# Loading the keys of a batch key head by key head in the second attention of a two-layer transformer

## What is computed

```
draft = einsum('bhqd,bhkd->bhqk', qr, kr) + causal
_, idx = top_k(draft, 128)
mask = full(neg); mask[idx] = 0; mask = where(future, neg, mask)
attn = softmax(draft / sqrt(16) + mask)
out = (attn @ v) @ Wo.T
```

## Time and profile before

| | |
|---|---|
| median of three runs | 2333.65 us |
| profiled execution | 2337.67 us |
| its span | 2335.8 us |
| TensorE busy | 1884.8 us, 81% |
| VectorE busy | 1568.4 us, 67% |
| ScalarE busy | 1180.0 us, 51% |
| GpSimd busy | 791.7 us, 34% |
| second attention with items 0 to 15 | about 1137 to 2109 us of the span |

### The profile page before, as it was taken

The page is one execution under the profiler, slowest core; times in us unless marked ns, Lnnn a source line. Parts: engine busy times, 40 slices in busy tenths (PEclk is TensorE's granted clock), DMA queues, the critical chain, the costliest instruction groups (busy, mean ns, idle before and its releaser), DMA issues. The chain is left out here.

```text
span 2335.8 us, 27456 instructions
## 1 busy us (share of the span) xinstructions
PE 1884.8 (81%) x8426; PEld 1377.3 (59%) x8426; DVE 1568.4 (67%) x3640; ACT 1180.0 (51%) x2963; POOL 791.7 (34%) x511
## 2 busy tenths in 40 slices
PE   5899999899998689997557776855877777677997
PEld 4777777777777568886534443432544434345885
DVE  3677777777777645556337888967888987822335
ACT  3556556556565332323355667645666676152221
POOL 3445545445454246553310111130211111132442
PEclk9999999999999889998756689977878887887998
DMA  4112111121110122221710000023000000001111
GB/s 154 32 44 69 66 51 54 52 79 49 43 65 24 62 81 88 101 81 58 134 29 14 15 14 1 1 28 41 5 16 9 14 15 14 1 1 46 55 41 50
DMA packets 48261, 104.71 MB, mean 45 GB/s; under 512 B 6032, under 2 KB 30992, under 8 KB 43664
## 3 DMA queue, kind: packets, MB, share of 16 engines
q1 hardware_dynamic: 48144, 103.40, 14.9%
HBM read 96.04 MB, written 7.34 MB: 44 GB/s over the span
## 5 line engine op out<-in xcount | busy, mean ns | idle before, releaser
L206 PE MATMUL PS<-XT,AR 128*128 128x512 f32 x2472 | 619.3, 405 | 25.7 <-POOL AR L813 12.3
L206 PE MATMUL PS<-AR 128*128 128x512 f32 (+2 forms) x2568 | 544.0, 366 | 24.8 <-POOL AR L323 13.1
L206 PEld LDWEIGHTS PS<-XT,AR 128*128 128x128 f32 x2472 | 470.6, 193 | 138.6 <-issue 16.5
L206 PEld LDWEIGHTS PS<-AR 128*128 128x128 f32 x2568 | 443.9, 193 | 119.5 <-issue 16.8
L1274 POOL TENSOR_TENSOR AF<-AF 128x512 f32<-128x512 f32 (+3 forms) x64 | 148.4, 2319 | 773.8 <-DVE AF L1474 773.8
L1229 ACT ACTIVATE AF<-PS 128x512 f32<-128x512 f32 x160 | 91.8, 596 | 329.7 <-PE PS L1113 190.0
L1416 DVE MAX8 BF<-PS 128x8 f32<-128x256 f32 (+2 forms) x384 | 195.8, 552 | 33.5 <-PE PS L1103 22.1
L1082 PE MATMUL PS<-AR,XT 48*128 48x128 f32 (+3 forms) x256 | 95.1, 458 | 146.1 <-DVE BF L1340 53.4
L1128 PE MATMUL PS<-AF,BF 128*128 128x512 f32 x320 | 190.9, 707 | 24.3 <-ACT AF L1229 24.3
L567 POOL TENSOR_TENSOR AF<-AF 128x512 f32<-128x512 f32 (+1 forms) x64 | 107.5, 1680 | 168.5 <-DVE AF L698 168.5
L1082 PEld LDWEIGHTS PS<-AR,XT 48*128 48x128 f32 x256 | 52.3, 243 | 185.2 <-issue 76.2
(11 more groups left out here) (173 smaller groups left out, 3516.4 us busy)
## 6 DMA issues: line engine op xcount, KB each, us to landing
AF<-in_mean_w SPq DMA_DIRECT2D x48, 448.0 KB, 3.3
AF<-in_ffn_w SPq DMA_DIRECT2D x14, 1536.0 KB, 6.5
AF<-in_attn_w SPq DMA_DIRECT2D x9, 1536.0 KB, 7.4
XT<-rope_scratch SPq DMA_DIRECT2D x192, 64.0 KB, 2.9
AF<-in_attn_w SPq DMA_DIRECT2D x9, 1024.0 KB, 5.2
AF<-in_ffn_w SPq DMA_DIRECT2D x11, 769.0 KB, 4.2
rope_scratch<-BF SPq DMA_DIRECT2D x20, 256.0 KB, 2.3
AR<-rope_scratch SPq DMA_DIRECT2D x24, 128.0 KB, 4.9
```

The source lines that it names most:

```text
L206: last = nc.tensor.matmul(dst, lhs(a, c), rhs(m, c), start=(first and k == 0), stop=(k == 3 * n - 1 and not more))
```

## The change

SyncE asks for an item's queries first and then for its keys, where before the keys came first. The keys are loaded key head by key head: for each of the four g, SyncE waits until head 4g+3 of the item two before has read its keys (`keys_read(x - 2, 4g + 3)`), and then issues six transfers of 32 KB. So each of items 0, 1, 8 and 9 has 24 key transfers and not 6. Each key head has a semaphore of its own; TensorE waits for it at each `scores(x, q)`, and GpSimd waits for all four before it negates.

```diff
-        def keys_read(x):
+        def keys_read(x, h=15):
 
-            return (listed(x, 15, 1) if tile_of(x)[1] > 0 else scored(x, 15)) + 1
+            return (listed(x, h, 1) if tile_of(x)[1] > 0 else scored(x, h)) + 1
...
                 if x >= 3:
                     sp.wait_ge(A1["ring_full"], keys_read(x - 3))
-                if n % QT == 0:
-                    if x >= 2:
-                        sp.wait_ge(A1["ring_full"], keys_read(x - 2))
-                    for low in (0, 64):
-                        for a, s in enumerate((0, 1, 0)):
-                            src = scr[b, 4, s].rearrange("(c h) t -> c h t", c=HD1)
-                            sp.dma_start(f32(kst[low + a * HD1:low + (a + 1) * HD1, 4 * hf:4 * hf + 4]),
-                                         src[:, 4 * hf:4 * hf + 4]).then_inc(A1[f"kst{hf}"], 16)
                 for low in (0, 64):
                     for j in range(2):
                         for a, s in enumerate((0, 0, 1)):
                             src = scr[b, 2 * hf + j, s].rearrange("(c h) t -> c h t", c=HD1)
                             sp.dma_start(f32(qst[x % 3][low + a * HD1:low + (a + 1) * HD1, 8 * j:8 * j + 8]),
                                          src[:, :, i * P:(i + 1) * P]).then_inc(A1[f"qst{x % 3}"], 16)
+                if n % QT == 0:
+                    for g in range(4):
+                        if x >= 2:
+                            sp.wait_ge(A1["ring_full"], keys_read(x - 2, G1 * g + G1 - 1))
+                        for low in (0, 64):
+                            for a, s in enumerate((0, 1, 0)):
+                                src = scr[b, 4, s].rearrange("(c h) t -> c h t", c=HD1)
+                                sp.dma_start(f32(kst[low + a * HD1:low + (a + 1) * HD1, 4 * hf + g]),
+                                             src[:, 4 * hf + g]).then_inc(A1[f"kst{hf}{g}"], 16)
...
+                pe.wait_ge(A1[f"kst{hf}{q}"], 96 * (n // QT + 1))
                 if q == 0:
-                    pe.wait_ge(A1[f"kst{hf}"], 96 * (n // QT + 1))
                     pe.wait_ge(A1[f"qst{x % 3}"], 16 * 12 * (x // 3 + 1))
...
-                pool.wait_ge(A1[f"kst{hf}"], 96 * (b + 1))
+                for g in range(4):
+                    pool.wait_ge(A1[f"kst{hf}{g}"], 96 * (b + 1))
```

More of the change, by code:

```diff
@@ L965, in build_kernel @@
         A1 = names("a1", "raw_qkv", "raw_wo", "wq_hi", "wq_lo", "wk_hi", "wk_lo", "wv_hi", "wv_lo", "wo_hi", "wo_lo",
-                   "tables", "vproj", "v", "vz", "stored0", "stored1", "kst0", "kst1", "qst0", "qst1", "qst2", "mask", "mask_r",
+                   "tables", "vproj", "v", "vz", "stored0", "stored1", "kst00", "kst01", "kst02", "kst03",
+                   "kst10", "kst11", "kst12", "kst13", "qst0", "qst1", "qst2", "mask", "mask_r",
                    "ring_full", "ring_free", "kneg", "above", "tiny", "stat", "nmax", "thr", "acc", "cut", "tau",
```

## The result

The kernel after takes 2328.20 us, the median of 12 runs (2323.24 to 2332.74), beside 2337.33 us for twelve runs of the kernel before (2333.04 to 2345.21): a ratio of 0.9958 [0.9944, 0.9971], or 9.8 us less [6.8, 13.1]. Run again in the study (`a1_after_again`) it gave 0.9952 [0.9931, 0.9974]. The profiled execution took 2323.24 us with a span of 2321.4, so 14.4 us less in both than the profiled one of before.

What follows compares the result with a forecast made beforehand. Second attention was taken as bound by TensorE's two in-order stalls on loads at the change of batch. -22.8 + 10.1 = -12.7 us from 2337.67 gives 2325.0; lowered by 4.0 for the runs' median, 2321 us, range 2313.5 to 2329.5.

Steps and rivals of the forecast that it cites:

- The stalls: Items 8 and 9, change of batch: TensorE's two waits for loads go, 10.25 and 12.58 us, together -22.8 us.
- Rival (d): Change of batch: a transfer or the score-bank ring still holds `scores(8, 0)`, one stall stays; 2331 to 2334 us; chance 0.05.
- The start: Batch 0: 72 transfers instead of 36 on SyncE's queue move `scores(2, 0)` from 1174.09 to 1184.2, +10.1 us.
- the spacing: SyncE's queue at the start: small key transfers issue 0.442 us apart, as the old ones; bounds 0.35 and 0.643.
- The reading that carried the sign: Start of the stage: transfer engines' time goes with the bytes, about 0.25 us for 32 KB against 0.98 for 128 KB.
- rival (b): Start: a small key transfer holds the engines as long as a large one; +9.6 us, 2343 us; chance 0.05.
- the backlog that was to disappear: Key transfers at the start: landings, up to 5.8 us behind issue before, come 2.8 us after issue.
- (a): Start: small transfers issue 0.35 us apart, so it costs only 5.7 us; -17.1 us, 2316.5 us; chance 0.13.
- (c): Start: small transfers issue 0.643 us apart like the query's, costing 19.8 us; -3.0 us, 2330.6 us; chance 0.07.
- Passed on in full: From `scores(2, 0)` to item 2's search: TensorE's order leaves no idle time, so all +10.1 us arrives.
- The small edits: More waits on TensorE, GpSimd and SyncE, 36 more issues under lists at the batch change: 0, at worst 1 us.
- 3 us of clock: TensorE's granted clock behind the removed stalls: counted 0, with 3 us kept for the range's fast end.

Runs made afterwards that it cites:

- e7: Changed kernel with batch 0's key transfers halved again, 48 of 16 KB per item: 1.0056 of the kernel before.
- e3: Changed kernel with two key heads per transfer at batch 0, 12 of 64 KB per item: 0.9902 of the kernel before, 0.9898 when run again.
- e1: Changed kernel with batch 0 loaded as before the change, batch 1 as after it: 0.9906 of the kernel before, 22.0 us less.
- e2: Changed kernel with batch 1 loaded as before the change, batch 0 as after it: 1.0057 of the kernel before, 13.3 us more.
- b1: Changed kernel whose start leaves out unread query rows and loads upper key rows later: 0.9884 of the kernel before, 0.9897 when run again.
- b2: The lean-start kernel (unread query rows left out, upper key rows later) with GpSimd's negation cut into one per key head: 0.9896 of the kernel before.
- e4: Kernel before with only the order changed at batch 1, queries ahead of whole keys: 0.9934 of the kernel before, 15.4 us less.
- e5: Kernel before with only the split at batch 1, key head by key head ahead of the queries: 0.9989 of the kernel before, 2.6 us less.
- e6: Changed kernel with batch 0's keys in six 128 KB transfers per item, issued by ScalarE's queue: 0.9938 of the kernel before, 14.5 us less.

## Why the prediction was right

**The stalls.** -22.8 was forecast. The waits of the two casts fell by 22.83 us, and the two intervals by 22.67 (19.6 to 24.0 in the other executions with both parts of the edit). Every step held: the scores behind the last list, cast 1.10 us behind the last instruction of `cut`, `scores(8, 1)` 7.4 us behind the cast (6.8 forecast). ScalarE's count for item 7 ended at 1541.14, 4.2 us behind the cast and ahead of the transposes, so nothing took the stalls' place. Rival (d) fell.

**The start.** +10.1 was forecast, +11.3 measured. The mis-sized term is the spacing: from the first key issue to the next query issue 24 transfers take 1156.36 - 1145.09 = 11.27 us, 0.470 each and not 0.442; 48 x 0.028 = 1.3 us covers the difference. The trace of before had it. I divided the first of its two groups at the start by six and left out the gap behind it; the second group is longer:

```profile
1148.12 2.90 SPq L1039 DMA_DIRECT2D AR<-rope_scratch  x6
1151.06 24.30 SPq L1045 DMA_DIRECT2D XT<-rope_scratch  x38
```

From the start of a key group to the start of what follows, (1140.37 - 1137.68 + 1151.06 - 1148.12) / 12 = 0.469 us.

The reading that carried the sign, that a small transfer doesn't hold the engines as a large one does, was right, and too cautious (1.9 us to land, not 2.8): rival (b), which needed 0.78 us each and landings that climb, fell with the change's own rows (0.47 us apart, 2.6 us at most to land) and again with e7, which halved the transfers without any backlog. That 12 of the 36 more issues were nearly free was inside the forecast, in the backlog that was to disappear; e3 shows it. Neither (a) nor (c) came: the form issues in 0.42 us at the median, as the old one did.

**Passed on in full.** The prediction argued this from TensorE's own order; e1, e2, e3 and e7 show it for a start from +0.3 to +33.8 us, within the 4 to 5 us of their intervals.

**The small edits** at 0: items 2 to 5 pass their casts in 0.86 us less than before, so 48 met waits of TensorE cost nothing that shows. The negation of item 1's keys is done at 1176.82 + 5.36 = 1182.18 (forecast 1182), before item 2's scores. It was hidden, but not without effect, which the prediction didn't see: VectorE's instruction of 16 elements was held for 2.61 us and ended 0.03 us behind it. It cost nothing because TensorE waited for item 2's queries until 1185.03; in b1, with a shorter start, a hold of this kind, 5.30 us long, cost about 3.5 us (32.8 against 29.2 in b2).

**The sum.** -12.7 against a profiled -14.4 and a measured -9.8 [-13.1, -6.8]. With the measured start it is -22.8 + 11.3 = -11.5, inside the intervals of both measurements. Of the profiled -14.4 some 3 us lie in stretches for which the prediction had counted 0 (-0.86 in items 2 to 5, -2.1 behind the change of batch); it had kept 3 us of clock for the range. The absolute time, 2321.0 forecast and 2328.2 measured, is 7.2 off, and half of that is not the change: I moved the sum down by 4.0 us for a median of three runs of before, and the median of twelve is 2337.33, at the profiled execution. The profiled execution of after is the fastest of its twelve, which is why it shows more than the medians do. The measured time lies only 1.3 us inside the upper end of the range (2329.5), an end that was set for rival (c), which didn't come: with a base 3.7 us too low the absolute time came close to falling outside, although the mechanism held. The difference to before is the better test, and there the forecast lies 2.9 us from the measured value, inside its interval.

## What to carry to other kernels

- A wait on one product may be a wait on what is queued ahead of it: read the in-order engine's last instruction before the gap, not the releaser's name, and ask which transfers stand behind the buffer's last reader.
- Splitting a load pays where its issues lie under other work. Where they don't, it is free only until the queue and no longer the transfers is the limit, and costs one issue each from there on. Split for the one place, keep it whole for the other; move first what depends on nobody, as order alone gave 13 of the 23 us, and the split alone 3 to 4.
- A spacing is read over all groups of its kind, from the start of one to the start of what follows: the first group alone was 6% short.

## What the runs showed of the hardware

- A second issuing queue added no bytes: 130 and 115 GB/s with two, 132 with one. Item 0's queries landed up to 14.1 us behind their issue and not 5.8. The same key transfers took 0.61 us each to issue on ScalarE's queue, beside 0.42 on SyncE's.
- The busy share of the transfer engines doesn't go with the bytes: from 1144 to 1154 it was 1.20 at 132 GB/s before, with keys of 128 KB, and 0.48 at 125 GB/s in e3, with keys of 64 KB. Why wasn't examined.
- A VectorE instruction of 16 elements in each partition was held for 5.30 us beside a GpSimd instruction of 5.4 us (5.19 when run again), 2.64 us in the kernel after and 1.04 in the kernel before, which met its later part; each time it ended 0.03 us behind it. Alone it takes 0.17. With the negation cut in four it took 0.36 and 0.17 us and ended inside a piece. The four took 12.43 / 2 = 6.2 us, 0.8 more than one.
- The granted clock comes back at different times in runs with nearly the same work. In e3, then in e1:

```profile
1240.00:1250.00 10.00, 8.56 (x56) 5.66 (x56) 8.46 (x35) 10.00 (x39) 0.00 (x0) 1.00 0.01 2
```
```profile
1240.00:1250.00 10.00, 9.31 (x35) 5.37 (x35) 6.06 (x25) 9.54 (x36) 0.00 (x0) 0.50 0.01 2
1250.00:1260.00 10.00, 10.00 (x43) 6.72 (x42) 9.07 (x33) 7.18 (x28) 0.00 (x0) 0.50 0.00 0
1260.00:1270.00 10.00, 9.51 (x44) 6.71 (x42) 5.34 (x18) 5.25 (x19) 0.00 (x0) 0.80 0.02 7
```

TensorE was busy for 9.31 us of e1's first ten and stayed at the low level. From item 2's scores to the first cast e3, before and after take 95.2 to 95.3 us, the repeats of e3 and after too; e4 takes 93.8, e1, e2, e5 and e6 100.2 to 100.4, and b1, b2 and e7 98.0 to 98.3 (for b2 3.1 us more than before, under half of the 6.9 by which its sum above is too large). Which start gives which I can't say: e3's start is 0.7 us off e1's. The shift from 0.79 to 0.86 behind the change of batch is likewise open. It goes with the stalls: all executions without one show it (0.83 to 0.87) but e7, and none with one does (0.77 to 0.80); no experiment was made on its cause. Each moves one execution by up to 5 us, so a single trace of this kernel gives a term of the sum and not the sum.
